# The attention weights turned in halves: 64 queries by 128 keys on two row halves of TensorE

## The reference, cut to what matters

```python
h = shift_token(x)
q, k, v = jnp.split(h @ wqkv, 3, axis=-1)              # 8 heads of 64
q = l2norm(q) * qs; k = l2norm(k) * ksc
q, k = rotary_xpos(q, k)
# windows of 128 queries; each sees its own 128 keys and the 128 before
sim = jnp.einsum('bhwid,bhwjd->bhwij', bq, bk)         # 128 x 256 a window and head
sim = jnp.where(mask, -jnp.finfo(sim.dtype).max, sim)
attn = jax.nn.softmax(sim, axis=-1)
out = jnp.einsum('bhwij,bhwjd->bhwid', attn, bv)
x = x + o @ wo
h = (layer norm of shift_token(x)) @ w1 + b1
a, g = jnp.split(h, 2, axis=-1)
x = x + (a * jax.nn.gelu(g)) @ w2 + b2
```

## Time and profile before

| | |
|---|---|
| median of 3 runs (lowest to highest) | 2856.45 us (2856.03 to 2857.04) |
| the profiled execution, and its span | 2855.33 us, 2853.2 us |
| PE busy | 2750.0 us, 96% |
| DVE, ACT, POOL busy | 2325.1 us (81%), 2284.3 us (80%), 1637.9 us (57%) |
| mean granted clock of TensorE | 0.988 |
| chain that ended last | PE 84%, DVE 8%, no cause shown 3% |

### The profile page before, as it was taken

The page is one execution under the profiler, slowest core; times in us unless marked ns, Lnnn a source line. Parts: engine busy times, 40 slices in busy tenths (PEclk is TensorE's granted clock), DMA queues, the critical chain, the costliest instruction groups (busy, mean ns, idle before and its releaser), DMA issues.

```text
span 2853.2 us, 75604 instructions
## 1 busy us (share of the span) xinstructions
PE 2750.0 (96%) x27108; PEld 2496.1 (87%) x27108; DVE 2325.1 (81%) x6459; ACT 2284.3 (80%) x5557; POOL 1637.9 (57%) x1652
## 2 busy tenths in 40 slices
PE   7999948999999999999999999999999999999998
PEld 6888836899999999999999899899999999999998
DVE  3979978988888888888888787888888888888884
ACT  4979956788888888888888788888888888888885
POOL 2323317666666666666666565666666666666653
PEclk9999979999999999999999999999999999999999
DMA  3252111121121112111111213111111111111111
GB/s 101 65 186 72 40 59 58 51 57 57 48 55 53 48 55 57 57 50 53 53 50 50 85 57 102 50 50 50 46 50 47 49 46 48 50 50 50 50 39 46
DMA packets 211334, 166.75 MB, mean 58 GB/s; under 512 B 21522, under 2 KB 206612, under 8 KB 209940
## 3 DMA queue, kind: packets, MB, share of 16 engines
q1 hardware_dynamic: 139284, 127.82, 14.8%
q10 hardware_dynamic: 71680, 34.10, 4.2%
HBM read 110.89 MB, written 42.58 MB: 54 GB/s over the span
## 4 chain that ended last, share of the span: by engine, by line
PE 84%; DVE 8%; issue 3%; ACT 2%; DMA 2%; SPq 1%; POOL 1%; ACTq 0%; DVEq 0%; POOLq 0%
PE ps L397 31%; PE ps L396 17%; PE ps L363 10%; PE ps L472 7%; PE ps L460 6%; PE ps L488 4%; DVE Sm L1112 3%; PE ps L445 3%; PE ps L498 2%; DVE Ar L1083 1%; DVE oTl L1135 1%; PE ps L524 1%; PE ps L423 1%; DMA oF<-ro_scratch 1%; PE ps L350 1%
## 5 line engine op out<-in xcount | busy, mean ns | idle before, releaser
L761 ACT ACTIVATE Sm<-Sm,nb 128x256 f32<-128x256 f32 (+1 forms) x1024 | 503.1, 496 | 1.4 <-DVE nb L1112 0.7
L1112 DVE CUSTOM_DVE_ANT_0 Sm<-ps,mask,sc 128x256 f32<-128x256 f32 (+1 forms) x1024 | 420.3, 475 | 77.3 <-PE ps L460 37.7
L1257 POOL TENSOR_TENSOR rs<-rs,mhalf 128x8 f32<-128x8 f32 x256 | 422.1, 1649 | 14.2
L1345 POOL TENSOR_TENSOR uTl<-Gl,uTh 128x512 fp32r<-128x512 f32 (+1 forms) x192 | 212.1, 1105 | 327.8 <-ACT uTh L834 219.7
L396 PE MATMUL ps<-zTh,W1h 128*128 128x256 f32 (+1 forms) x1408 | 375.6, 288 | 0.1
L741 ACT ACTIVATE sq<-ps 128x512 f32<-128x512 f32 x256 | 151.5, 592 | 269.4 <-PE ps L397 265.7
L396 PE MATMUL ps<-zTh,W1l 128*128 128x256 f32 (+1 forms) x1408 | 365.7, 282 | 0.0
L1184 DVE SCALAR_TENSOR_TENSOR Gl<-ps,vecs,Gl 128x256 f32<-128x256 f32 (+1 forms) x384 | 172.0, 476 | 219.8 <-PE ps L396 118.8
L397 PE MATMUL ps<-WQh,hTh 128*128 128x512 f32 x768 | 339.3, 442 | 2.8 <-ACT hTh L735 2.8
L397 PE MATMUL ps<-WQl,hTh 128*128 128x512 f32 x768 | 302.9, 394 | 0.0
L1356 POOL TENSOR_TENSOR Ar<-Ar,Br 128x512 f32<-128x512 f32 x128 | 164.6, 1286 | 219.9 <-DVE Br L1085 219.9
(11 more groups left out here) (190 smaller groups left out, 8645.7 us busy)
## 6 DMA issues: line engine op xcount, KB each, us to landing
oF<-ro_scratch ACTq DMA_DIRECT2D x256, 128.0 KB, 3.1
tb<-tab SPq DMA_DIRECT2D x128, 128.0 KB, 2.3
xc<-x SPq DMA_DIRECT2D x32, 256.0 KB, 3.0
rwkv_scratch<-rw SPq DMA_DIRECT2D x32, 256.0 KB, 2.7
rk<-rwkv_scratch SPq DMA_DIRECT2D x64, 128.0 KB, 2.3
xin<-x SPq DMA_DIRECT2D x64, 128.0 KB, 2.3
x_scratch<-x SPq DMA_DIRECT2D x64, 128.0 KB, 1.7
y_scratch<-os SPq DMA_DIRECT2D x64, 128.0 KB, 4.2
```

The costliest lines, as they stand in the source:

```text
L761: act.activation(Sm[:, h, c0:c1_], Sm[:, h, c0:c1_], ACT.Exp, bias=nb[:, h:h + 1], scale=-1.0, accum_out=sm[:, n % 2, h:h + 1]).then_inc(S ...
L1112: dve.tensor_tensor_reduce(Sm[:, h, c0:c1_], PS[:, bank["scores", n, q, h % 2], (h // 2 % 2) * 256 + c0:(h // 2 % 2) * 256 + c1_], mask[:, ...
L1257: return pool.tensor_tensor(ap, ap, mhalf[:, 0:ap.shape[-1]], ALU.pow)
L1345: pool.tensor_tensor(uT[1][:, j, :], Gl[:, g, :], uT[0][:, j, :].bitcast(F32), ALU.subtract).then_inc(S["ul"], 1)
```

## The change

P is turned by 64 queries and 128 keys at a time: the stationary operand is `Sm` on 64 partitions, the identity is 64 x 64. The halves r = 0 and r = 1 alternate. A call of `turn_p` now takes four heads and both halves, 16 transposes, into two banks, one for each half; there are two calls a unit, where the two runs were. The banks' number and place in the ring stay. ScalarE reads each bank with one copy as before, and writes it to the columns of `PT` that belong to the half. The semaphore p5 counts runs and no longer banks. In all the step loops the two kinds of steps are now written apart (`if t % 2 == 0`), with the same order of calls otherwise.

```diff
@@ psum_order2
-    if live(5):
-        yield "turn", t - 5, 0
-        yield "turn", t - 5, 1
+            yield "turn", t - 5, 0, 0
+            yield "turn", t - 5, 0, 1
...
-        yield "turn", t - 5, 2
-        yield "turn", t - 5, 3
+            yield "turn", t - 5, 1, 0
+            yield "turn", t - 5, 1, 1
@@ read_out
             if what == "turn":
-                return S["pt"], 4 * n + i[0] + 1
+                return S["pt"], 4 * n + 2 * i[0] + i[1] + 1
@@ tensor_program
             def turn_p(n, j):
-                c0, c1_ = cols(n)
-                k = bank["turn", n, j]
-                w.wait_ge(S["ex"], 8 * n + 2 * j + 2)
-                w.wait_ge(*read_out(former["turn", n, j]))
-                for i in range(2):
-                    for c in range(c0, c1_, 128):
-                        ins = pe.transpose(PS[:, k, i * 256 + c:i * 256 + c + 128], Sm[:, 2 * j + i, c:c + 128],
-                                           ident[:, :])
+
+                sides = [n % 2] if first_win(n) else [0, 1]
+                w.wait_ge(S["ex"], 8 * n + 4 * j + 4)
+                for r in range(2):
+                    w.wait_ge(*read_out(former["turn", n, j, r]))
+                for h in range(4):
+                    for s in sides:
+                        for r in range(2):
+                            rows = slice(64 * r, 64 * r + 64)
+                            at = h * 128 + s * 64
+                            ins = pe.transpose(PS[:, bank["turn", n, j, r], at:at + 64],
+                                               Sm[rows, 4 * j + h, s * 128:(s + 1) * 128], ident[rows, rows])
                 ins.then_inc(S["p5"], 1)
@@ scalar_program
-            def p_out(n, j):
-                c0, c1_ = cols(n)
-                w.wait_ge(S["p5"], 4 * n + j + 1)
-                w.wait_ge(S["p6"], 2 * (n - 1) + j // 2 + 1)
-                act.activation(PT[:, 2 * j:2 * j + 2, c0:c1_],
-                               PS[:, bank["turn", n, j], :].rearrange("p (h j) -> p h j", h=2)[:, :, c0:c1_],
+            def p_out(n, j, r):
+                sides = slice(n % 2, n % 2 + 1) if first_win(n) else slice(0, 2)
+                w.wait_ge(S["p5"], 2 * n + j + 1)
+                w.wait_ge(S["p6"], 2 * (n - 1) + j + 1)
+                act.activation(PT[:, 4 * j:4 * j + 4, :].rearrange("p h (s t) -> p h s t", s=2)[
+                                   :, :, sides, 64 * r:64 * r + 64],
+                               PS[:, bank["turn", n, j, r], :].rearrange("p (h s t) -> p h s t", h=4, s=2)[:, :, sides, :],
                                ACT.Copy).then_inc(S["pt"], 1)
@@ vector_program, masked_max
-                    w.wait_ge(S["p5"], 4 * (n - 1) + h // 2 + 1)
+                    w.wait_ge(S["p5"], 2 * (n - 1) + q + 1)
```

More of the change, by code:

```diff
@@ L135, in psum_order2 @@
[L135 to L148, removed]
+    if t % 2 == 0:
+        if live(6):
+            yield "pv", t - 6, 0
+            yield "pv", t - 6, 1
+        if live(7):
+            yield "wo", t - 7
+        if live(11):
+            yield "gate", (t - 11) // 2, 0
+            yield "up", (t - 11) // 2, 0
+        if live(5):
+            yield "turn", t - 5, 0, 0
+            yield "turn", t - 5, 0, 1
+        if live(11):
+            yield "gate", (t - 11) // 2, 1
+            yield "up", (t - 11) // 2, 1
+        if live(5):
+            yield "turn", t - 5, 1, 0
+            yield "turn", t - 5, 1, 1
+        if live(11):
+            yield "gate", (t - 11) // 2, 2
+            yield "up", (t - 11) // 2, 2
+        if live(4):
+            yield "scores", t - 4, 0, 0
+            yield "scores", t - 4, 0, 1
+            yield "scores", t - 4, 1, 0
+            yield "scores", t - 4, 1, 1
+        if live(2):
+            yield "qkv", t - 2, 1
+        if live(5):
+            yield "rT", t - 5
+        if live(3):
+            yield "qkT", t - 3, 1
+        if live(2):
+            yield "qkv", t - 2, 0
+        if live(3):
+            yield "qkT", t - 3, 0
+        if live(2):
+            yield "qkv", t - 2, 2
+        if live(1):
+            yield "hT", t - 1
+        if live(10):
+            yield "zT", t - 10
+        if live(0) and t < NG:
+            yield "pre", t
+    else:
+        if live(6):
+            yield "pv", t - 6, 0
+            yield "pv", t - 6, 1
+        if live(7):
+            yield "wo", t - 7
+        if live(10):
+            yield "zT", t - 10
+        if live(13):
+            yield "w2", t - 13
+        if live(5):
+            yield "turn", t - 5, 0, 0
+            yield "turn", t - 5, 0, 1
+        if live(12):
+            yield "w2", t - 12
+        if live(5):
+            yield "turn", t - 5, 1, 0
+            yield "turn", t - 5, 1, 1
+        if live(4):
+            yield "scores", t - 4, 0, 0
+            yield "scores", t - 4, 0, 1
+            yield "scores", t - 4, 1, 0
+            yield "scores", t - 4, 1, 1
+        if live(2):
+            yield "qkv", t - 2, 1
+        if live(5):
+            yield "rT", t - 5
+        if live(3):
+            yield "qkT", t - 3, 1
+        if live(2):
+            yield "qkv", t - 2, 0
+        if live(3):
+            yield "qkT", t - 3, 0
+        if live(2):
+            yield "qkv", t - 2, 2
+        if live(1):
+            yield "hT", t - 1
+        if live(0) and t < NG:
+            yield "pre", t
@@ L569, in live @@
                     return 0 <= t - d < U
[L571 to L599, removed]
@@ L839, in live @@
                     return 0 <= t - d < U
[L841 to L869, removed]
@@ L1201, in live @@
                     return 0 <= t - d < U
-                odd = 1 - t % 2
-                if live(9):
-                    z_norm(t - 9)
-                if live(8):
-                    z_stats(t - 8)
-                if live(6):
-                    o_norm(t - 6)
-                if live(7):
-                    x2_out(t - 7)
-                    zero_h2(t - 7)
-                if live(5):
-                    o_sums(t - 5)
-                if live(11) and odd:
-                    glu((t - 11) // 2, 0)
@@ L1217, in vector_program @@
-                if live(12) and not odd:
-                    x3_out(t - 13)
-                if live(11) and odd:
-                    glu((t - 11) // 2, 1)
-                if live(12) and not odd:
-                    x3_out(t - 12)
-                if live(11) and odd:
-                    glu((t - 11) // 2, 2)
-                if live(4):
-                    masked_max(t - 4, 0)
-                    masked_max(t - 4, 1)
-                if live(1) and t - 1 < NG:
-                    pre_y(t - 1)
```

370 lines of the change are left out of this document (263 added, 107 removed).

## The result

| | before | after |
|---|---|---|
| median of 5 runs (lowest to highest) | 2856.40 us (2855.97 to 2857.04) | 2843.03 us (2842.20 to 2843.97) |
| ratio to before (95%) | | 0.9952 (0.9941 to 0.9963) |
| span of the profiled execution | 2853.2 us | 2840.9 us |
| mean granted clock | 0.988 | 0.986 |

A forecast was written before the change was run, and what follows sets the result against it. TensorE (PE) was taken to bound the kernel, with VectorE nearly a second bound in the first layer. Savings of 14.4 + 21.1 us by layer, -1.6 for first windows, +1.5 for first steps, gave 35 us: 2821 us, range 2808 to 2861.

The forecast's parts named there:

- The pair, the load, the switches: PE's half-height transposes: 0.057 us a pair, loads occupying the array about 0.056, 0.14 to enter row halves, 0.19 to leave.
- the first rival: Transposes on PE: a 128-column load sets the pair at 0.109 to 0.118 us, giving 2939 us; 16%.
- A middle run: Transpose run with full-array work on both sides: 0.79 us against 0.87, 0.08 saved, three times a pair of steps.
- The run before the scores: Second transpose run of odd steps, next to row-half scores: 0.65 us against 1.07, 0.42 saved.
- PE's own saving: PE's time in a pair of steps: 3 x 0.08 + 0.42 = 0.66 us saved.
- The first layer's 0.45: First-layer pair of steps: 0.45 of the 0.66 us survives, 0.40 from VectorE's loop plus 0.05 from a shorter load.
- the cap: First layer: odd-step scores wait for VectorE's x2 write, so the loop has only 0.40 us to give, plus 0.05.
- the same write: Second layer: x2's write ends 1.3 us before the odd step's scores, so all 0.66 us a pair survives.
- ScalarE's reads of PSUM (L768): ScalarE's four copies of transposed P: shorter write runs priced at nothing, first read of a run nothing to 0.1 us later.
- The first steps: Steps before there is an MLP: two adjacent runs share a switch, 5 x 0.3, a gain of 1.5 us.
- Switches at the dear end: Row-half switches 0.19 us in and out, 0.06 a pair; a middle run hardly gains, 2832 us; 20%.
- No cap: First layer: VectorE's loop has more slack than it shows, so 64 x 0.66 = 42 us saved, 2814 us; 10%.

The follow-up runs named there:

- e3: Changed kernel with VectorE instead of ScalarE making one of the four PSUM copies of a unit, in the second layer's odd steps; 2836.70 us.
- e4: Changed kernel with half-height transposes only in the second run of odd steps, whole ones in the three other runs; 2844.99 us.
- e7: Changed kernel with the first transpose run of odd steps moved behind the second w2 matmul, beside the second run; 2835.54 us.
- e8: e5, e6 and e7 together: first 12 units whole, three of four runs beside the scores; 2813.76 us.
- e6: Changed kernel with the second transpose run of even steps moved behind the third MLP part, right before the scores; 2824.33 us.
- e5: Changed kernel with whole transposes and a wait for each head's exponential in the first 12 units; 2838.24 us.
- e1: Changed kernel's grouping (four heads a run, one wait) but with all transposes whole, 128 x 128; 2860.17 us.
- e2: Changed kernel with a wait for each head's exponential, not one for four heads, in the first eight units; 2842.05 us.
- e9: e8 with VectorE's o_norm cut in two and x2 written between the halves; 2823.07 us.
- e10: e8 with half-height transposes and one wait for four heads from the first unit on; 2816.55 us.

## Why the prediction was right and wrong

**The pair, the load, the switches: right.** Pairs follow every 0.062 us (1208.340 to 1208.651 for the last six of a run), where 0.057 was taken; the extra 0.05 before the second pair belongs to entering. The load takes 140 ns as before, and the first rival, a pair at 0.109 to 0.118, did not come. By the rule of the Trainium skill (TensorE: Matmul & The Clock Gate, section LDWEIGHTS), the load's columns over 1.2 GHz or 107 ns a load, these pairs could not follow at 0.062; the trace does not agree with it here. Entering costs 0.14 (taken: 0.14), leaving 0.20 (taken: 0.19).

**A middle run: right in direction, half the size.** 0.08 was forecast. The even step, with two of them, gave 0.075 (21.346 to 21.272, and 20.118 to 20.042), so 0.04 a run. Eight pairs at 0.062 instead of 0.057 account for 0.04 of it.

**The run before the scores: nearly right.** 0.42 forecast; from the last two w2 matmuls to the second pair of the scores PE takes 1.05 us instead of 1.43 (medians, both layers), 0.38 less.

**PE's own saving: 0.47 a pair of steps, not 0.66.** This is what both layers give where nothing stands in the way (after, first layer; e3, second layer). The middle runs at half their forecast size and the last run's 0.38 make most of the difference; the odd step's middle run gave 0.03 (e4 against after, first layer). It is the mis-sized term of the sum: 29 x 0.19 = 5.5 us of those missing in the second layer.

**The first layer's 0.45: right by luck.** 0.466 was measured, but this is PE's own saving and not a cap on a larger one: the second layer gains the same 0.47 once its stall is gone. The wait named as the cap does exist. From x2's write to the scores were 0.56 us before and 0.17 after, and it stops only what came on top, down to 0.10 in e7 and e8. Two errors met: the saving was taken 0.19 too large, and the cap was set against the whole pair, where e6 shows that it holds the odd step's saving alone.

**"In the second layer the same write ends at 2204.01 and the scores start at 2205.32, 1.3 us later, enough for all of it": wrong.** This is the step that failed. It asked whether the bank that bounds the first layer bounds the second too, and not which bank comes next there. The scores take several; the second half's is the first turn bank of the same step, and ScalarE, which has its own order (four exponentials, the z outputs, then this copy), was done with it 0.44 us before the half began. The prediction had "ScalarE's reads of PSUM (L768) stay four of 128 x 512"; it priced their length and the start of the first, and not who waits for their end. Two edits that share nothing, another engine for the copy (e3) and another place of its transposes (e7), give the same 35.97 and 35.96. The second layer at 0.25 instead of 0.66 is 29 x 0.41 = 12 of the 22 us missing: 6 to 7 by this wait (e3 is 6.3 us faster than after), the rest by PE's smaller saving. The eleven steps around the change of layer gave 0.2 instead of some 2, which stays open.

**The first steps: wrong in sign.** The sum gave them +1.5 for a shared switch. The four at the full clock gave 0.8; the two at a lowered clock took 5.0, and 1.5 more came ahead of them: 5.7 lost where 1 to 3 were to be won, some 8 of the 22; the 1.5 stem from the first stage, as said under e5. The prediction took the full clock of the steady steps for the whole run and had no term for the clock. That the clock is most of the price is shown, by the steps it falls in and by the table above. The coarse wait alone does not bring it down: e1 has one short stretch, and e2 with fine waits has the full two. The half-height transposes in the first units go with it, by the mean clock of 28 executions against 24. How they do it stays open, and chance has a part: e5 and e8, the same code up to there, differ.

**The rivals.** "Switches at the dear end" gave 2832 and would have been nearest in number. Half of its reason held: leaving costs 0.20 and a pair 0.062, as it had them, but entering 0.14 and not 0.19. "No cap" could not show itself in this change, since PE's own saving was too small; e7 and e8, which save more, meet the cap.

## What to carry to other kernels

When an edit shortens one engine's run, list for the next instruction every bank and semaphore that it waits for, with the time at which each was ready, for each stage of the kernel by itself: the gain ends at the second latest, not at the one you know. Work in a tiling mode of its own is best put next to other work in that mode: two lines moved on top of the change were worth more (e6, 18.7 us) than the new shape itself (13.4). A forecast that is right in number for one stage can be so by two errors: check it against a stage or a run where the cap is gone. Look at the first steps by themselves, and at the granted clock in each.

## What the runs showed of the hardware

- fp32 transposes of 64 rows run on the two row halves at the same time, a pair every 0.062 us, with loads of 140 ns each.
- An excursion of the transposes into row halves costs 0.33 us (0.14 in, 0.20 out), and neighbours in the same mode share it (e6, both layers).
- From the end of the write or read that frees a bank to the start of the matmul that waited lie 0.10 us (e7, e8) to 0.15 (after and e7, second layer: 0.14 and 0.15).
- Moved by one place, a VectorE multiply grew from 0.69 to 1.26 us beside GpSimd (e9).
- The granted clock falls to one half for 3.4 or 6.8 us at a time in the first steps, in other places and numbers from kernel to kernel. A step with 6.8 us of it is 2.1 to 3.0 us longer than before (after, e2, e3, e6, e7, e10), one with 3.4 us 1.2 to 1.7 (e1, e4, e5, e7).
- Half-height transposes in the first units go with a lower mean clock: 0.9855 over 28 executions, against 0.9875 over 24 with whole ones.
